# Second biases moved from TensorE matmuls to GpSimd and VectorE in a cross-attention and mixture-of-experts kernel

## The reference

```python
h = tanh(txt_proj[:, None, :, :] + feat_proj[:, :, None, :] + b)      # 4 x 1024 x 77 x 256
rho = einsum('bftd,d->bft', h, w); att = softmax(rho masked)          # ...
x = x + (w_s * features + b_s)
# feed-forward, on the layernorm of x
scores, token_idx = top_k(flat_probs, k=512)                          # per expert
h = gelu(einsum('ecd,edh->ech', tok, W1) + b1[:, None, :])
out_tok = einsum('ech,ehd->ecd', h, W2) + b2[:, None, :]
scaled = out_tok * scores[..., None]
routed = zeros.at[token_idx].add(scaled)
shared = einsum('gsh,hd->gsd', gelu(einsum('gsd,dh->gsh', x, Ws1) + bs1), Ws2) + bs2
x = x + routed + shared
```

## Time and profile before

| | |
|---|---|
| median of 3 runs | 874.42 us |
| the profiled execution's own time | 874.54 us |
| its span (first to last instruction) | 872.8 us |
| granted TensorE clock, mean | 0.988 |
| PE busy | 787.4 us (90%) |
| ACT busy | 752.9 us (86%) |
| DVE busy | 716.1 us (82%) |
| POOL busy | 285.3 us (33%) |

### The profile page before, as it was taken

How to read it: one execution, slowest core, us unless ns; L and a number is a source line. 1 busy time by engine, 2 the same in 40 slices (tenths; PEclk the granted TensorE clock), 3 DMA queues, 4 the chain that set the end, 5 groups by cost and what they waited for, 6 DMA issues and landing times.

```text
span 872.8 us, 13908 instructions
## 1 busy us (share of the span) xinstructions
PE 787.4 (90%) x5385; PEld 473.5 (54%) x5385; DVE 716.1 (82%) x1426; ACT 752.9 (86%) x554; POOL 285.3 (33%) x388
## 2 busy tenths in 40 slices
PE   7875588569998999999999999998999999999996
PEld 6221133124443345454445545554777999999986
DVE  4789899997888999998989999995787776666541
ACT  4999999999999999999999999987754676767672
POOL 3100430341523007653002700063504145555424
PEclk9899999999999999999999999999999999999999
DMA  8000000000001000200000010002203355554513
GB/s 263 28 0 1 1 1 1 1 25 25 2 1 49 1 1 25 73 2 1 25 1 1 25 50 1 25 2 78 92 25 97 129 138 146 145 136 103 137 20 41
DMA packets 32405, 41.81 MB, mean 48 GB/s; under 512 B 2365, under 2 KB 29011, under 8 KB 32339
## 3 DMA queue, kind: packets, MB, share of 16 engines
q1 hardware_dynamic: 26083, 32.49, 11.5%
q0 software_dynamic: 6144, 8.39, 5.5%
q10 hardware_dynamic: 112, 0.04, 0.0%
HBM read 28.33 MB, written 12.58 MB: 47 GB/s over the span
## 4 chain that ended last, share of the span: by engine, by line
ACT 38%; PE 37%; DVE 12%; issue 8%; POOL 3%; DMA 1%; ACTq 0%; POOLq 0%; DVEq 0%
ACT z L1042 35%; PE bank L954 10%; PE bank L977 9%; DVE z L1434 8%; PE bank L828 5%; PE bank L885 4%; PE bank L870 2%; ACT u L1096 2%; POOL y_ry L1169 2%; PE bank L754 1%; PE bank L803 1%; PE bank L992 1%; PE bank L928 1%; DMA vec_rows<-in_L_xattn_w_dram 1%; POOL xn L1176 1%
## 5 line engine op out<-in xcount | busy, mean ns | idle before, releaser
L1042 ACT ACTIVATE z<-z 128x4096 f32<-128x4096 f32 (+5 forms) x157 | 536.2, 3484 | 4.8 <-DVE z L1434 4.6
L1434 DVE TENSOR_SCALAR z<-feat,txt_bias 128x1024 f32<-128x1024 f32 (+1 forms) x760 | 434.8, 647 | 17.4 <-PE bank L828 17.0
L828 PE MATMUL bank<-z,window 128*32 128x512 f32 x2464 | 296.5, 608 | 56.9 <-ACT z L1042 55.1
L828 PEld LDWEIGHTS bank<-z,window 128*32 128x32 f32 x2464 | 68.7, 110 | 239.4 <-issue 136.0
L885 PE MATMUL bank<-ws_sb,u 128*128 128x256 f32 x512 | 124.7, 386 | 2.0 <-ACT u L1096 2.0
L885 PEld LDWEIGHTS bank<-ws_sb,u 128*128 128x128 f32 x512 | 92.6, 190 | 34.6 <-issue 18.1
L870 PE MATMUL bank<-tr,ws_s 128*128 128x512 f32 x384 | 108.2, 419 | 2.0 <-ACT u L1096 2.0
L954 PE MATMUL bank<-xg_s,w_s 128*128 128x512 f32 x384 | 99.1, 396 | 0.3 <-DVE xg_s L1790 0.2
L1796 DVE TENSOR_TENSOR hid_s<-hid,hid_s 128x512 fp32r<-128x512 f32 x60 | 41.5, 692 | 59.3 <-ACT hid_s L1142 48.0
L977 PEld LDWEIGHTS bank<-w_s,hid_s 128*128 128x128 f32 x672 | 86.3, 188 | 3.9
L977 PE MATMUL bank<-w_s,hid_s 128*128 128x256 f32 x672 | 88.1, 280 | 0.0
(11 more groups left out here) (263 smaller groups left out, 728.4 us busy)
## 6 DMA issues: line engine op xcount, KB each, us to landing
w_raw<-in_L_ffn_W_dram SPq DMA_DIRECT2D x16, 1024.0 KB, 5.6
x_ring<-in_x_dram SPq DMA_DIRECT2D x8, 512.0 KB, 8.0
xn_dram<-xn SPq DMA_DIRECT2D x8, 512.0 KB, 2.9
out_dram<-x_ring SPq DMA_DIRECT2D x8, 512.0 KB, 2.9
u<-in_L_ffn_Ws_dram SPq DMA_DIRECT2D x1, 1024.0 KB, 11.3
ws_sb<-in_L_ffn_Ws_dram SPq DMA_DIRECT2D x1, 1024.0 KB, 14.0
xg<-xn_dram,idx POOLq DMA_INDIRECT x32, 3.2
out_dram<-y,idx POOLq DMA_INDIRECT x32
```

The costliest lines, as they stand in the source:

```text
L828: ins = e.matmul(sums[v][32 * g:32 * g + 32, :], window[:, c, 31 - at_row:63 - at_row], z[:, n % ZB, at_piece:at_piece + TOK], start=(v, g ...
L1042: e.activation(part, part, ACT.Tanh).then_inc(signal(*step), 1)
L1434: ins = e.tensor_scalar(z[:, n % ZB, i * width:(i + 1) * width], feat_of(units, c), bias_of(units, t, c), None, ALU.add)
```

## The change

Both second biases leave TensorE: the 32 matmuls of L881, the 28 of L971 and the 4 of L987, with `split_b2`, its tiles, its four loads and its clearing, are gone. The first matmul of each sum now starts the bank itself.

For bs2, SyncE loads the row into all partitions (`bs2_rep`, 128 x 256), and a new GpSimd step `biased` behind the four `whole` of a unit adds it to the unit's four rows of `x_ring`; `down_end` waits for `biased` in place of `whole`.

For b2, SyncE loads all eight rows into all partitions (`b2_rep`, 128 x 2048, 1 MB written), behind the weights of expert 0. A new GpSimd step `bias_rows(ex)` multiplies the row of the expert with each tile's score (4 instructions of 128 x 256). `e_out` moves from ScalarE to VectorE, as one instruction per tile: sum times score plus bias row.

```diff
-    at_slots(0, (8,), [[("split_b2",)]])
-                *[[("y_turned", v, c)] for c in range(C)], [("whole", v, j) for j in range(J)]]
+                *[[("y_turned", v, c)] for c in range(C)], [*(("whole", v, j) for j in range(J)), ("biased", v)]]
-              ("load_w1", 0), ("load_w2", 0), *end[2], ("att_exp", vb), ("early_probs",)]
+              ("load_w1", 0), ("load_w2", 0), ("load_b2",), *end[2], ("att_exp", vb), ("early_probs",)]
+        if m == 3:
+            steps.append(("bias_rows", ex))
...
 @@ SyncE
-            e.wait_ge(consts, B2_CLEAR)
-            for first in (0, B2_LOW):
-                e.dma_start(b2_raw[first:first + E, :], b2).then_inc(loaded["b2"], 16)
-                e.dma_start(b2_raw[first + E:first + E + 1, :], bs2.unsqueeze(0)).then_inc(loaded["b2"], 16)
+            e.dma_start(bs2_rep[:], bs2.partition_broadcast(P)).then_inc(loaded["bs2"], 16)
+                elif kind == "load_b2":
+                    e.wait_ge(*done("rho_turn", vb))
+                    e.dma_start(b2_rep[:], b2.rearrange("e d -> (e d)").partition_broadcast(P).rearrange("p (e d) -> p e d", e=E)
+                                ).then_inc(loaded["b2"], 16)
...
 @@ TensorE, e_down (down and e_tile in the same way)
-                        for a in range(A):
-                            e.matmul(sums_of[a // 2][:, a % 2 * D:(a % 2 + 1) * D], b2_row[:, ex:ex + 1].broadcast_to([B2_ROWS, P]), b2_s[:],
-                                     start=a % 2 == 0, stop=False, skip_group_check=True)
-                                           start=False, stop=(m == M - 1 and term == 2), skip_group_check=True)
+                                           start=m == 0 and a % 2 == 0 and term == 0, stop=(m == M - 1 and term == 2),
+                                           skip_group_check=True)
...
 @@ GpSimd
+                elif kind == "biased":
+                    e.wait_ge(loaded["bs2"], 16)
+                    for j in range(J):
+                        row_of = x_ring[:, v % XB, j, :]
+                        e.wait_ge(*done("whole", v, j))
+                        ins = e.tensor_tensor(row_of, row_of, bs2_rep[:], ALU.add)
+                    ins.then_inc(signal(*step), 1)
+                elif kind == "bias_rows":
+                    e.wait_ge(loaded["b2"], 16)
+                    e.wait_ge(*done("scored", ex))
+                    if ex > 1:
+                        e.wait_ge(*done("e_out", ex - 2, A - 1))
+                    for a in range(A):
+                        ins = e.tensor_scalar(bias_rows[:, ex % 2, a, :], b2_rep[:, ex, :], score[:, ex % NL, a:a + 1], None, ALU.mult)
+                    ins.then_inc(signal(*step), 1)
...
 @@ e_out, ScalarE
-                    e.activation(y[:, ex % 2, a, :], banks[bank][:, left:left + D], ACT.Identity,
-                                 scale=score[:, ex % NL, a:a + 1]).then_inc(signal(*step), 1)
 @@ e_out, VectorE
+                    e.wait_ge(*done("bias_rows", ex))
+                    e.wait_ge(*(done("e_sum", ex, a // 2) if ex < E - 1 else done("e_tile", a)))
+                    e.scalar_tensor_tensor(out=y[:, ex % 2, a, :], in0=banks[bank][:, left:left + D],
+                                           scalar=score[:, ex % NL, a:a + 1], in1=bias_rows[:, ex % 2, a, :], op0=ALU.mult,
+                                           op1=ALU.add).then_inc(signal(*step), 1)
```

More of the change, by code:

```diff
@@ L379, in work_order @@
         order += up(E - 1, m)
+        if m == 3:
+            order.append(("bias_rows", E - 1))
     for a in range(A):
@@ L539, in xattn_moe_kernel @@
         high, remainder, within, *passed = [hid_flat[:, i * NH * P:(i + 1) * NH * P] for i in range(8)]
-        assert cursor[0] <= early_end, (cursor[0], early_end)
+        assert cursor[0] <= b2_at and b2_at + E * D * 4 <= rows_at and rows_at + 2 * A * D * 4 <= early_end
+        b2_rep = sb("b2_rep", [P, E, D], at=b2_at)
+        bias_rows = sb("bias_rows", [P, 2, A, D], at=rows_at)
         xg_s = sb("xg_s", [P, 2, 2, C, TOK], F32R, at=tr_at)
@@ L592, in xattn_moe_kernel @@
         }
-        BY_DMA = ("load_x", "load_w1", "load_w2", "store_xn2", "store_out", "gather", "scatter")
+        BY_DMA = ("load_x", "load_b2", "load_w1", "load_w2", "store_xn2", "store_out", "gather", "scatter")
         count, at = {}, {}
@@ L621, in xattn_moe_kernel @@
         loaded = {name: semaphore(f"ld_{name}") for name in
-                  ["w", "ctx", "ws", "vec", "mask", "bc", "gate", "ws1", "ws2", "b2", *(f"x{v}" for v in range(UNITS)),
+                  ["w", "ctx", "ws", "vec", "mask", "bc", "gate", "ws1", "ws2", "b2", "bs2", *(f"x{v}" for v in range(UNITS)),
                    *(f"{name}_{ex}" for name in ("w1", "w2") for ex in range(E))]}
@@ L876, in _ @@
                         e.wait_ge(loaded["ws2"], 16)
-                        e.wait_ge(*done("split_b2"))
                     if m == 0:
[L879 to L882, removed]
+                        for j in range(first + first % 2, end, 2):
+                            take(DOWN[j // 2])
                     e.wait_ge(*done("gelu", v, m))
@@ L885, in _ @@
                         ins = e.matmul(banks[DOWN[j // 2]][:, j % 2 * D:(j % 2 + 1) * D], u[:, m % UR, j * P:(j + 1) * P],
-                                       ws2_sb[:, m, :], start=False, stop=m == M - 1, skip_group_check=True)
+                                       ws2_sb[:, m, :], start=m == 0 and j % 2 == 0, stop=m == M - 1, skip_group_check=True)
                     ins.then_inc(signal(*step), 1)
@@ L986, in _ @@
                     part = (banks[LAST_SUM[a]] if a < 2 else take(LAST_SUM[a]))[:, 0:D]
-                    e.matmul(part, b2_row[:, ex:ex + 1].broadcast_to([B2_ROWS, P]), b2_s[:], start=True, stop=False)
                     for m in range(M):
@@ L992, in _ @@
                             ins = e.matmul(part, slice_of(ex, m)[:, i, a * P:(a + 1) * P], w2_s[ex % 2][:, j, m, :],
-                                           start=False, stop=m == M - 1 and term == 2)
+                                           start=m == 0 and term == 0, stop=m == M - 1 and term == 2)
                     ins.then_inc(signal(*step), 1)
@@ L1142, in _ @@
                     e.activation(slice_of(ex, m)[:, 0, :], hid[:, m % HC, :], ACT.Copy).then_inc(signal(*step), 1)
-                elif kind == "e_out":
-                    ex, a = args
-                    bank, left = (SUM[ex % 2][a // 2], a % 2 * D) if ex < E - 1 else (LAST_SUM[a], 0)
-                    e.wait_ge(*(done("e_sum", ex, a // 2) if ex < E - 1 else done("e_tile", a)))
-                    e.wait_ge(*done("scored", ex))
-                    if ex > 1:
-                        e.wait_ge(scattered, 16 * A * (ex - 1))
-                    e.activation(y[:, ex % 2, a, :], banks[bank][:, left:left + D], ACT.Identity,
-                                 scale=score[:, ex % NL, a:a + 1]).then_inc(signal(*step), 1)
         @block.gpsimd
@@ L1646, in _ @@
                     e.wait_ge(*done(*summed[v, half]))
-                    e.wait_ge(*done("whole", v, J - 1))
+                    e.wait_ge(*done("biased", v))
                     xs = x_ring[:, v % XB, 2 * half:2 * half + 2, :].rearrange("p j d -> p (j d)")
@@ L1791, in _ @@
                                     ALU.subtract).then_inc(signal(*step), 1)
+                elif kind == "e_out":
+                    ex, a = args
+                    bank, left = (SUM[ex % 2][a // 2], a % 2 * D) if ex < E - 1 else (LAST_SUM[a], 0)
+                    e.wait_ge(*done("bias_rows", ex))
+                    e.wait_ge(*(done("e_sum", ex, a // 2) if ex < E - 1 else done("e_tile", a)))
+                    e.wait_ge(*done("scored", ex))
+                    if ex > 1:
+                        e.wait_ge(scattered, 16 * A * (ex - 1))
+                    e.scalar_tensor_tensor(out=y[:, ex % 2, a, :], in0=banks[bank][:, left:left + D],
+                                           scalar=score[:, ex % NL, a:a + 1], in1=bias_rows[:, ex % 2, a, :], op0=ALU.mult,
+                                           op1=ALU.add).then_inc(signal(*step), 1)
                 elif kind == "e_lo":
@@ L1796, in _ @@
                     e.tensor_tensor(parts[:, 1, :], hid[:, m % HC, :], parts[:, 0, :].bitcast(F32),
-                                    ALU.subtract).then_inc(signal(*step), 1)
-                elif kind == "split_b2":
-                    low = slice(B2_LOW, 2 * B2_LOW)
-                    e.wait_ge(loaded["b2"], 64)
-                    e.tensor_tensor(b2_row[:], ident[0:B2_ROWS, 0:E + 1], ident[0:B2_ROWS, B2_LOW:B2_LOW + E + 1], ALU.add)
-                    link(e.tensor_copy(b2_s[:], b2_raw))
-                    e.wait_ge(vector_link, linked)
-                    e.tensor_tensor(b2_s[low, :], b2_raw[low, :], b2_s[low, :].bitcast(F32),
                                     ALU.subtract).then_inc(signal(*step), 1)
```

15 lines of the change are left out of this document (6 added, 9 removed).

## The result

The changed kernel takes 881.99 us (median of 6 runs, 881.1 to 883.76) against 874.41 for the kernel before on the same chip: ratio 1.009, 95% interval 1.0074 to 1.0106. It is slower; forecast was 871.0.

A forecast was written before the change was run, and what follows sets the result against it. ScalarE bounds the tanh stage and TensorE alone the experts. Off 3.29 + 0.48 + 0.24 + 0.20 = 4.21 us, on 0.8, net 3.4: 871.1 us from the profiled 874.54, 871.0 against the median; range 869.7 to 873.3.

The forecast's parts named there:

- Bias matmuls of the experts: At seven expert takeovers, removing the bias matmuls of experts 0 to 6 saves 0.47 us of chain each, 3.29 us.
- The last expert: In the last expert, bias matmuls of four row tiles leave the chain at 0.12 us each, saving 0.48 us.
- Unit 7's matmuls: Of unit 7's four shared-network bias matmuls, two are in the chain at 0.12 us; saving taken as 0.24 us.
- split_b2's 0.20: Taking split_b2 off VectorE at 58 us saves only ScalarE's 0.20 us wait for an add at 72.16.
- e_out and bias_rows: Experts: four e_out on VectorE (1.6 to 1.9 us) and bias_rows on GpSimd (2.2 to 5.3 us) fit idle gaps, cost 0.
- rival B: Experts: VectorE late at the takeover, e_lo slips over 2 us, TensorE waits the gain away; 874.4 us; chance 0.07.
- rival C: GpSimd's adds of unit 2 shut out, x_norm of unit 6 ends 9 us late; 876.0 us; chance 0.04.
- VectorE loses 0.39/2.73 = 14% for as long as GpSimd works: Tanh stage, z adds beside `biased`: VectorE slows by 14% while GpSimd works, taken as 4.6 us per unit.
- units 2 to 5: The new adds cost 0.4 us in units 3 and 2 and 0.4 us in units 4 and 5.
- Units 0 and 1 ... 0: Near 250 us the adds cost 0, as VectorE has 15 us to spare from 155 to 335 us.
- Units 6 and 7 ... 0: The adds of these units stand behind the z adds or beside the search and cost 0.
- Rival A: z adds beside GpSimd's adds: VectorE blocked for whole instructions, 0.55 us per add, 7.0 us lost; 877.2 us; chance 0.05.

The follow-up runs named there:

- Experiments 2 and 3: Changed kernel with `biased`'s tensor_tensor adds replaced by tensor_scalar instructions: four per unit (2), ratio 0.9974; eight per unit (3), ratio 0.9965; shared bias left out.
- experiment 9: Changed kernel plus filler matmuls in two TensorE gaps: four ahead of unit 4's router matmuls, five ahead of the search's fourth total; ratio 1.0043 against 1.0085 unfilled.
- the experts' half: Kernel before with only bias_rows, load_b2 and e_out on VectorE; split_b2 and the 32 bs2 matmuls kept; run twice, ratios 0.9972 and 0.9958.

## Why the prediction was wrong

**Bias matmuls of the experts: right.** 0.47 to 0.48 us at each of seven takeovers, 3.35 in all against 3.29.

**The last expert: right in sign, too high.** 0.25 us at the end, not 0.48. The first e_out there waited 3.4 us for bias_rows (I had written some 2), and the chain that ended last now holds three scatters from 867.82 on, where before it held one; what each of these took was not tried.

**Unit 7's matmuls: 0.43 against 0.24.** split_b2's 0.20 can't be told: the profiled executions differ by -1.3 to +1.9 us from that of before by 200 us, whatever the kernel.

**e_out and bias_rows: right.** 1.65 us for four (1.6 to 1.9), 0.52 us left in the gap (0.4); rival B is out. A row of four bias_rows took 5.26 us (2.2 to 5.3), its start at 768.59, next gather at 777.32. x_norm of unit 6 ended at 387.56, some 3 us later than I wrote, and rival C's shut-out didn't occur there.

**The step that failed** is the last of the part by part: "VectorE loses 0.39/2.73 = 14% for as long as GpSimd works". That rate was read under `whole`, a tensor_scalar, and carried over to a tensor_tensor, of which I had said that the trace has no row. Experiments 2 and 3 show that the two forms behave in opposite ways in these places: the one yields to VectorE and stretches itself, the other halves VectorE's speed or stops it. For units 2 to 5 I had 0.8 us; it was 4.0, after the 1.2 won before 502 us. GpSimd was busy there to 516.7, where I had written 511 or so; my own 4.6 us a unit would have made it 513. "Units 0 and 1 ... 0" rested on VectorE's 15 us to spare in 180; but what waited was a single feat behind twenty z adds (10.47 and 6.68 us instead of 8.70 and 5.38), and TensorE behind it: 3.16 us. "Units 6 and 7 ... 0" overlooked that in the search VectorE's small steps are themselves the chain: 3.67 us. In both places I priced no fall of TensorE's clock, 2.7 us of the 6.7 by experiment 9.

**Rival A was the mechanism**, given 0.05. Its 0.55 us per add times 16 less leads was 7.0 us; measured were 4.0 for those units and 6.8 at the places that it left out. The Trainium skill (SBUF — State Buffer, "SBUF: two separate sides") has the rule of an exclusive lock, with the loser blocked for the whole instruction. The trace agrees in the search, and goes further, since the 2.95 us span four adds. Under the adds of units 4 and 5 it agrees in part: z adds and GpSimd's adds go one for one, but four such pairs took 3.56 us (from 513.43), where a z add alone (0.41 us, 16 in 6.61 in the trace of before) and a GpSimd add (0.70, 2.79/4 in the search) in turn would be 4.4. It disagrees for tensor_scalar, under which VectorE lost 1.6 us in 32.2. I had taken one row against the rule as enough to drop it, though that row was of the other form.

**What the change didn't cause.** 1.66 of the profiled 7.77 us, at 599 to 611, come in 6 of 13 profiles, with and without adds, with and without bs2 matmuls: a wait of TensorE of 2.0 us, behind which it falls to 1.2 GHz or doesn't. The rest is 10.8 us on and 4.7 off (the small changes between the stretches included), 6.1 net. The timings say 4.6 off without the adds (0.9947) and, for the whole change, 7.4 on (1.0085, from 5.6 to 9.3).

## What to carry to other kernels

Before work goes to GpSimd beside a busy VectorE, look for a row of the same form, not of the same size: with a second tile as input it cost VectorE here about a third of its own duration (9.6 us in 29.3), and a chain of small VectorE steps all of it. "VectorE has room in this stage" says nothing on one instruction that another engine waits for; follow who waits for the steps that stand beside the new ones. Removing matmuls from a full TensorE paid their time in the chain (3.35 us for 3.29), where what replaced them had a gap of its own.

## What was not expected of the hardware

- GpSimd's tensor_tensor and VectorE: z adds of 128 x 512 at a median of 966 ns against 482; a 128 x 7 instruction held for 2.95 us against 0.23, to the end of four adds. The reverse stands in the same traces: the 128 x 4 power on GpSimd of the earlier trace rows took 15.35 to 15.37 us in 12 of the 14 traces, up to the end of a row of z adds, though it is itself a tensor_tensor: the form alone doesn't say who yields.
- The same instruction took 1.50 us in the other two, one of them the experts' half, which had 15.37 in its second; the wait of TensorE for y_norm was then gone, and the delay fell by 1.97 us. So a kernel has more than one course, by a race between two engines, and its time moves by 2 us with it. What decides it was not tried.
- TensorE fell to half its clock behind waits of 1.5 to 2.4 us, and not each time: the 16 router matmuls took 3.56, 3.50, 2.93, 2.24 and 1.92 us behind waits of 2.06, 2.05, 1.46, 2.06 and 2.05.
